# A graph layer on one core: node ranges of 64 that serve 512 edges of a group in place of 256

## What is computed

```
h = relu(layernorm(x))
msg = [h[dst], edge_attr]                       # 53125 x 128
e = relu(msg @ W1a.T + b1a) @ W1b.T + b1b
agg = segment_sum(e, src) / max(counts, 1)      # 3125 x 64
z = relu([h, agg] @ W2a.T + b2a) @ W2b.T + b2b
out = x + [z, h] @ Wr.T + br
```

## Time and profile before

| | |
|---|---|
| median of 3 runs | 522.17 us (521.17 to 524.77) |
| span of the profiled execution, first to last instruction | 518.3 us |
| what lies around the span, against the median | 3.9 us |
| TensorE busy | 431.0 us (83%) |
| VectorE busy | 298.0 us (57%) |
| ScalarE busy | 285.0 us (55%) |
| GpSimd busy | 356.1 us (69%) |

### The profile page before, as it was taken

How to read it: one execution, slowest core, us unless ns; L and a number is a source line. 1 busy time by engine, 2 the same in 40 slices (tenths; PEclk the granted TensorE clock), 3 DMA queues, 4 the chain that set the end, 5 groups by cost and what they waited for, 6 DMA issues and landing times.

```text
span 518.3 us, 9203 instructions
## 1 busy us (share of the span) xinstructions
PE 431.0 (83%) x3133; PEld 390.0 (75%) x3133; DVE 298.0 (57%) x825; ACT 285.0 (55%) x576; POOL 356.1 (69%) x406
## 2 busy tenths in 40 slices
PE   6655988899999999998689779845999787987795
PEld 4555777888796988878578778845998777987674
DVE  7868642534656657555425547414765537667884
ACT  3442957774787777786658378171633772100073
POOL 4777777777677777777777777777777777776000
PEclk9876696987999899988899889986999897999999
DMA  7998998553959477978553989996999997778631
GB/s 182 306 338 229 257 266 271 155 156 108 303 143 294 141 257 265 257 255 263 164 151 92 336 249 333 312 331 196 360 326 336 328 322 221 248 214 256 177 86 43
DMA packets 62319, 123.45 MB, mean 238 GB/s; under 512 B 9369, under 2 KB 33374, under 8 KB 62270
## 3 DMA queue, kind: packets, MB, share of 16 engines
q1 hardware_dynamic: 49598, 91.25, 59.0%
q0 software_dynamic: 12672, 31.58, 18.8%
HBM read 71.53 MB, written 51.25 MB: 237 GB/s over the span
## 4 chain that ended last, share of the span: by engine, by line
POOL 32%; PE 26%; DMA 13%; issue 13%; DVE 7%; ACT 5%; SPq 2%; POOLq 0%; ACTq 0%; DVEq 0%
POOL slots_dram L568 24%; PE bank L1261 10%; POOL pairs_dram L551 8%; DMA slots_dram<-pay,pos_i 7%; PE bank L1241 4%; PE bank L1270 4%; DMA dstb<-in_dst 4%; DVE oh L774 2%; DMA rows<-slots_dram 2%; ACT eo L1059 2%; SPq L475 1%; PE bank L1294 1%; PE bank L1291 1%; PE bank L1211 1%; PE bank L1362 1%
## 5 line engine op out<-in xcount | busy, mean ns | idle before, releaser
L568 POOL DMA_INDIRECT slots_dram<-pay,pos_i x300 | 289.0, 963 | 98.7 <-issue 89.6
L1261 PE MATMUL bank<-rows,oh 128*125 128x130 f32 x1100 | 139.5, 287 | 40.3 <-DVE oh L774 40.1
L1261 PEld LDWEIGHTS bank<-rows,oh 128*125 128x125 f32 x1100 | 133.3, 198 | 44.6 <-issue 43.4
L1059 ACT ACTIVATE eo<-dstb,minus_lane 64x256 f32<-64x256 int32 x190 | 85.1, 494 | 94.5 <-DMA dstb<-in_dst 79.8
L1241 PE MATMUL bank<-pw,eo 128*128 128x128 f32 x856 | 119.9, 299 | 3.5 <-ACT pay L1042 2.3
L1241 PEld LDWEIGHTS bank<-pw,eo 128*128 128x128 f32 x856 | 113.3, 213 | 11.4 <-issue 8.0
L774 DVE TENSOR_TENSOR oh<-bank,rows 128x1500 f32<-128x1500 f32 (+5 forms) x67 | 81.8, 1223 | 17.6 <-DMA rows<-slots_dram 10.4
L1270 PE MATMUL bank<-hid,xch 116*128 116x131 f32 (+1 forms) x512 | 68.3, 294 | 14.6 <-DVE xch L724 8.6
L1270 PEld LDWEIGHTS bank<-hid,xch 116*128 116x128 f32 (+1 forms) x512 | 65.3, 205 | 16.9 <-issue 9.9
L551 POOL DMA_INDIRECT pairs_dram<-pay,pos_c x64 | 61.5, 960 | 22.3 <-issue 18.0
L1064 ACT ACTIVATE eo<-eo,one 64x512 f32<-64x512 f32 x95 | 68.3, 719 | 3.1
(11 more groups left out here) (198 smaller groups left out, 376.7 us busy)
## 6 DMA issues: line engine op xcount, KB each, us to landing
rows<-slots_dram SPq DMA_DIRECT2D x24, 864.0 KB
dstb<-in_dst SPq DMA_DIRECT2D x54, 256.0 KB, 7.7
eo<-in_edges_T SPq DMA_DIRECT2D x54, 256.0 KB, 4.9
rows<-pairs_dram SPq DMA_DIRECT2D x12, 864.0 KB
slots_dram<-zeros SPq DMA_DIRECT2D x9, 756.0 KB, 9.2
slots_dram<-pay,pos_i POOLq DMA_INDIRECT x300
rows<-slots_dram SPq DMA_DIRECT2D x8, 432.0 KB
rows<-slots_dram SPq DMA_DIRECT2D x16, 216.0 KB
```

Of the source, the lines that this page charges most:

```text
L568: pool.indirect_dma_start(out=slots_dram[:, :], out_offset=bass.IndirectOffsetOnAxis(ap=pos_i[:, u, k:k + 1], axis=0), in_=pay[:, u, k, :] ...
L1059: last = A.activation(eo[p, g % EB, a * HB:(a + 1) * HB], dstb[p, g % DB // 2, a * HB:(a + 1) * HB], ACT.Square, bias=minus_lane[p, g // 2 ...
L1261: last = T.matmul(o[0:BN, v * SW:(v + 1) * SW], oh2[:, r % 2, n, :], rows[:, sum_no[r] % RR, n, 0:SW], start=(t == 0), stop=(t == TB[ph] - ...
```

## The change

A range of 64 nodes now serves 512 edges of a group (462 in a paired one): `HB` = 512, hence `KW` = 2. There are half as many projections and pieces, and the copy of the ranges has half the columns; the matmuls of `hidden` and their number are the same. `LEAD` goes from 26 and 30 to 18 and 22 nodes. The pad right of `hT` grows from 64 to 96 columns. Around it, the paired pairs get phases of their own (`PAIRED`), with just one in the list, so all the regions keep their sizes; the share of room after a paired group is now only lowered from group 10 on; and the check of the paired regions moves.

```diff
-    WS, HB = 64, 256
+    WS, HB = 64, 512
     KW = GE // HB
...
-    BLOCK = [HB if kind == "O" else UNIT for kind in ORDER]
-    LEAD = [26 if kind == "O" else 30 for kind in ORDER]
+    BLOCK = [HB if kind == "O" else 2 * UNIT for kind in ORDER]
+    LEAD = [18 if kind == "O" else 22 for kind in ORDER]
...
-        room = min(MOST, room + (C_SHARE if g - 1 in C_GROUPS else SHARE if g >= FULL_FROM else EARLY_SHARE))
+        room = min(MOST, room + (SHARES["after_paired" if g - 1 in C_GROUPS else "after_old"] if g >= FULL_FROM else EARLY_SHARE))
...
-                A.copy(pw[p, g % WB, :, :], bank[p, 7, :].rearrange("p (k h) -> p k h", h=HID)).then_inc(S["pc"], 1)
+                blocks = blocks_of(g // 2)
+                A.copy(pw[p, g % WB, 0:blocks, :], bank[p, 7, 0:blocks * HID].rearrange("p (k h) -> p k h", h=HID)).then_inc(S["pc"], 1)
...
-                for c in range(KW):
+                for c in range(blocks_of(i)):
                     n0 = PAD_L + window(i, c)
...
-                            pe.wait_ge(S["oha"], 2 * (g - ACT_FROM) + a // 2 + 1)
+                            pe.wait_ge(S["oha"], 2 * (g - ACT_FROM) + 2 * a // KW + 1)
...
-                split_row(c_parts, c_carry, 2 * SCALE * SCALE, S["cw"])
+                if n + 1 not in C_STARTS:
+                    split_row(c_parts, c_carry[:], 2 * SCALE * SCALE, S["cw"])
+                    return
+                p = C_STARTS.index(n + 1) - 1
+                check_chunks(p)
...
-            check_chunks()
             for r in left_over:
```

More of the change, by code:

```diff
@@ L67, in gnn_layer @@
     FIRST_GROUP = [2 * O_PAIRS[STARTS[ph]] for ph in range(NPH)] + [NG]
-    END_GROUP = [2 * O_PAIRS[STARTS[ph + 1] - 1] + 2 for ph in range(NPH)] + [2 * C_PAIRS[-1] + 2]
+    C_STARTS = [sum(PAIRED[:p]) for p in range(NCP + 1)]
+    assert C_STARTS[-1] == len(C_PAIRS)
+    FIRST_PAIRED = [2 * C_PAIRS[C_STARTS[p]] for p in range(NCP)]
+    END_GROUP = [2 * O_PAIRS[STARTS[ph + 1] - 1] + 2 for ph in range(NPH)] + [2 * C_PAIRS[C_STARTS[p + 1] - 1] + 2 for p in range(NCP)]
     def expected(ph):
@@ L96, in gnn_layer @@
     SCALE = 256
-    TB = C + [2 * CT]
+    TB = C + [2 * tiles for tiles in CT]
     X_PARTS = [(0, 2), (2, 9), (9, NB)]
@@ L113, in gnn_layer @@
     sum_rounds = []
-    for ph in sorted(range(NPH + 1), key=lambda ph: END_GROUP[ph] + AFTER_PHASE[ph]):
+    for ph in sorted(range(NPH + NCP), key=lambda ph: END_GROUP[ph] + AFTER_PHASE[ph]):
         m = min(512 // SW, TPR // TB[ph])
@@ L137, in gnn_layer @@
     room = 0
-    for g in range(NG):
+    for g in range(LG):
         units = [("perm", C_GROUPS.index(g - 1), u, 0) for u in range(UNITS)] if g - 1 in C_GROUPS else []
@@ L165, in gnn_layer @@
     round_of = {n: r for r, n in sum_no.items()}
-    first_round = [min(r for r, v in enumerate(rounds) if v[0] == "sum" and v[1] == ph) for ph in range(NPH + 1)]
+    first_round = [min(r for r, v in enumerate(rounds) if v[0] == "sum" and v[1] == ph) for ph in range(NPH + NCP)]
     last_perm = [rounds.index(("perm", c, UNITS - 1, 0)) for c in range(len(C_GROUPS))]
@@ L323, in gnn_layer @@
         s_sc = [sem(f"rows_scattered_{u}") for u in range(PB)]
-        s_cfill = sem("chunk_regions_cleared")
+        s_cfill = [sem(f"chunk_regions_cleared_{p}") for p in range(NCP)]
         s_sc2 = [sem(f"chunk_rows_scattered_{u}") for u in range(CR)]
@@ L344, in scatters_of @@
         def scatters_of(u, n):
-            return 16 * sum(KT[O_GROUPS[a]] for a in range(u, n, PB))
+            return 16 * sum(KT[O_GROUPS[a]] for a in range(u, min(n, len(O_GROUPS)), PB))
         def chunk_scatters_of(u, c):
@@ L460, in _ @@
             loaded = 0
-            for g in range(3, NG):
+            for g in range(3, LG):
                 if g >= 6:
@@ L468, in _ @@
                         clear(ph, piece)
+                for p in range(1, NCP):
+                    piece = len(CLEAR_PIECES) - (FIRST_PAIRED[p] - g) // 2
+                    if g % 2 == 0 and 0 <= piece < len(CLEAR_PIECES):
+                        clear_chunks(p, piece)
                 if g == CLEAR_FROM:
@@ L539, in _ @@
             count(unit_row[:], [[1, K + 1], [0, 2]], 0, 0)
-            count(c_first[:], [[C_CAP, NB]], C_BEGIN, 0).then_inc(S["late"], 1)
+            for p in range(NCP):
+                last = count(c_first[:, p, :], [[C_CAP[p], NB]], C_BEGIN[p], 0)
+            last.then_inc(S["late"], 1)
             pool.wait_ge(S["pad"], 1)
-            for g in range(NG):
+            for g in range(LG):
                 if g in C_GROUPS:
@@ L1098, in _ @@
             copy_window(4)
-            for g in range(3, NG):
+            for g in range(3, LG):
                 relu(g)
-                if g + 2 < NG:
+                if g + 2 < LG:
                     copy_window(g + 2)
@@ L1297, in sum_round @@
                     pe.wait_ge(S["bc"], 1)
-                    for a in range(4):
-                        last = T.transpose(o[0:1, a * NBK:(a + 1) * NBK], col_stat[:, a // 2, a % 2:a % 2 + 1], I[0:NBK, 0:NBK])
+                    for a in range(2):
+                        last = T.transpose(o[0:1, a * NBK:(a + 1) * NBK], col_stat[:, a:a + 1], I[0:NBK, 0:NBK])
                 last.then_inc(S["ag"], 1)
```

134 lines of the change are left out of this document (75 added, 59 removed).

## The result

The changed kernel takes 534.07 us (median of four runs, 533.97 to 534.75); the kernel before took 521.67 us on the same chip (four runs, 520.62 to 524.77). The ratio is 1.0233, with a 95% interval of 1.02 to 1.0266: the change is 2.3% slower. The forecast was 523.2 with a range of 518.0 to 526.7. The profiled execution took 534.15 us, with a span of 532.4 us.

A forecast was written before the change was run, and what follows sets the result against it. GpSimd was taken as the bound from 14 us on, at 1.264 us a step. Span 518.3 + 1.95 (TensorE late at C2) - 0.95 (check moved) = 519.3 us, median 523.2, range 518.0 to 526.7.

The forecast's parts named there:

- 0.4 forecast: At the start: the first scatter comes 0.4 us earlier, lost again at C1 and not in the sum.
- 3.87 forecast: Ahead of group 10's hidden rows, before C1: two moved "h" rounds add 3.87 us to TensorE.
- I take the same levels for the change.: Around C2: granted clock as before, 0.50 at 114 to 115 us within the "z" rounds, 1.00 again at 124.
- -1.5: Groups 6 to 11: ScalarE's savings move TensorE's chain from C0 on by -0.8 to -2.3 us, middle taken.
- my 101.5: C1: GpSimd starts it at 101.5 us in place of 101.33, after waiting for `pos_c`.
- +2.47: Behind group 11, before C2: five "h" matmuls and one "z" in place of four "h" add 2.47 us.
- +1.6: Between C1 and C2: net TensorE delay of 1.6 us from moved rounds, less half the projection.
- the 139: C3: forecast near 136.5 us; a start above 139 us would show the forecast wrong, by low clock.
- The slower rival: Group 12's rounds to C3's perm rounds: "z" block holds the clock low, +8.3 us, 531.5; chance 0.06.
- From group 16 on TensorE has less to do.: After C3: one sum round less there, half the projections, so GpSimd runs without a stop, carrying +1.95 us.
- -0.95: The end: `check_chunks` leaves its place ahead of the first left-over one-hot, saving 0.95 us; bounds -0.95 and 0.
- the last wait of that kind is at 427 us: Near the end: VectorE's last wait for a scatter's landing, 4.45 us at 427.25, for group 47's rows.

The follow-up runs named there:

- wide_old_plan: The change with its new rule for placing "h", "z" and sum rounds put back as before: 522.86 us against 521.43 for the kernel before, ratio 1.0025.
- z_later_calls_3: The change with the old round plan, clears and `xr` load called later, three "z" rounds moved from behind group 12 to 15 and 19: 523.16 us, ratio 1.0033.

## Why the prediction was wrong

**Right.** GpSimd is the bound, at 1.264 us a step; TensorE's and ScalarE's savings are covered, and by `wide_old_plan` the ranges are worth nothing in time that can be told (1.0025, 0.999 to 1.006). The first scatter came 0.46 us earlier (0.4 forecast) and this was lost again. `check_chunks` at the end was worth what was said: in `wide_old_plan` the left-over sums wait 0.71 us for their one-hot at 468.10 in place of 1.67, which is 0.96 against 0.95, and from the last wait for a landing (432.28) to the end it is 90.2 us (90.1 forecast). The two "h" rounds took 3.89 us (3.87 forecast). The waits came at C1, C2 and C3. A slip that changes nothing: 523.2 less 2.6 is 520.6, not 520.5.

**"I take the same levels for the change."** This is the step that failed first. The clock was weighed only behind the "z" rounds of group 12, not behind the two "h" rounds that the change puts ahead of C1. TensorE's chain from C0's perm rounds to the end of C1's is 4.18 us later at its end. It started 0.20 earlier (91.88 against about 92.08), the "h" rounds gave +3.69 (start to start), group 10's hidden rows +1.74, projection and wait together -1.73, and C1's perm rounds +0.68. So 1.74 and 0.68, and half of the projection's saving, are the clock, none of which was in the sum. The trace of before has rows that show it. There are two "h" rounds at 76.70 and 79.04 us, and behind them (granted clock 0.50 from 80 to 88 us):

```profile
80.96 2.02 PE L1241 MATMUL bank<-pw,eo 128*128 128x128 f32 x8
83.46 2.08 PE L1241 MATMUL bank<-pw,eo 128*128 128x128 f32 x8 [0.47 <-ACT hid L1042]
85.33 3.70 PE L1270 MATMUL bank<-hid,xch 116*128 116x131 f32 x16
```

These are 8, 8 and 16 passes, at 0.25, 0.26 and 0.23 us each in place of 0.12.

**"-1.5" for ScalarE's lead.** It did not come through; 0.2 did, and that by luck: C0's perm rounds started 2.95 us later than before (88.28 against 85.33) and were done earlier since they ran at the high clock, 3.77 us in place of 6.9 with a wait of 1.14 in it. The lead was there (in `wide_old_plan` the copy of hT that stood at 57.96 us comes at 54.12), but it ended at VectorE's wait for group 3's landing, and at TensorE's 8.59 us of waiting for `eq_c` at 70.06. My bounds for it, 0.8 to 2.3, did not hold zero. Together these two steps make C1 3.9 us later than my 101.5. Other traces bear this out for C1: the four with two "h" rounds ahead of it start C1 at 104.7 to 108.1 us, and of the six without, four at 101.3 to 102.2. The other two are `wide_old_plan` (105.56, low clock in the perm rounds) and `z_later_calls_3` (104.28, the late `xr`).

**"+2.47" ahead of C2.** From the end of C1's rounds to the start of C2's it is 3.80 us longer: the "h" and "z" part behind group 11 +3.76, as it includes a wait of 1.05 us for VectorE's `xr`; group 12's hidden rows +1.74 at the low clock; the "z" block -0.87, the projection -0.27, group 13's hidden rows -0.57. C2's own rounds then ran at the full clock, 3.77 us in place of 4.74. C2 came 3.0 us further behind than C1, where +1.6 was forecast. C3 at 141.5 lies beyond the 139 that the prediction had named as the sign of the low clock.

**The slower rival** had nearly the right time, 531.5, by another way: it put the low clock behind group 12's "z" block, on the perm rounds of C2 and C3. These took 3.77 and 3.84 us, at full clock. Its mechanism is refuted for this trace; that its number is near is a coincidence.

**"From group 16 on TensorE has less to do."** This is the second failed step, worth 4.84 of the 14.1 us (0.82 at C9, 4.02 at C11). The sum of the work is less, but I counted it over the whole stretch and did not look at what stands where the moved rounds went. The rounds that moved up ahead of C3 made room, and sum rounds moved into the places of "z" rounds directly behind a paired group's ranks. The wait that such a sum round has was to be seen in the trace of before, behind group 31's ranks:

```profile
257.01 5.23 PE L1261 MATMUL bank<-rows,oh 128*125 128x130 f32 x32 [4.64 <-DVE oh L774]
```

There it cost nothing: `pos_c` of C12 was ready at 273.6 us and GpSimd came to it at 281.3. One such round fits into the lead, a row of three does not.

**The end.** -0.95 was forecast, +2.25 came. The check's part was right; what was not in the sum is the wait for group 49's landing and 3.0 us of low clock behind it, and as two traces with the same plan have neither, whether it is the change's own stays open. I had written that the last wait of that kind is at 427 us and asked what is late behind the last scatter, not what is late between the two.

By the Trainium skill, "TensorE: Matmul & The Clock Gate", part 1 on the clock gate, sustained activity brings the high level; the prediction said that the trace speaks against it at 114 us, and the stretch from 95 to 100 us of the kernel after does again (TensorE without a gap since 77 us, granted 1.00 at 92 to 94 us and 0.50 here).

## What to carry to other kernels

A rule that sets where filler work goes is a change of its own: here it cost all of the 2.3%, while the edit named in the title gave nothing that could be told. When rounds move, price them at the place they come to, in three parts: their own time, what the next work costs if the clock is low behind them, and what they must wait for on another engine there. And a bound that rests on "there is room later" wants one look at each place where the order differs, not only at the first; the place with the largest single wait (4.0 us) was one that I had not looked at.
